# A routed feed-forward kernel on one core: three of batch 5's row scatters issued ahead of a weight split instead of behind it, in GpSimd's queue

## The reference

```python
x = x + attention(layernorm(x))       # one causal head, Wq, Wk, Wv (256 x 256), softmax(scores / 16)
x = x + ffn(layernorm(x))

def ffn(x):
    shared = down(silu(gate(x)) * up(x))                 # inner width 512
    probs = sigmoid(x @ router_w.T + routing_bias)       # 8 experts
    scores, indices = top_k(probs, 2); scores /= sum(scores)
    combined = sum over the 2 chosen experts of score * down_e(silu(gate_e(x)) * up_e(x))
    return shared + combined
```

## Time and profile before

| what | value |
|---|---|
| median of 3 runs | 569.48 us |
| lowest, highest | 565.53, 570.84 us |
| time of the profiled execution | 570.84 us |
| its span | 568.7 us |
| TensorE matmul busy | 519.9 us (91% of the span) |
| VectorE, ScalarE, GpSimd busy | 365.0, 301.2, 289.4 us |
| mean granted TensorE clock | 0.982 of full speed |

### The profile page before, as it was taken

One profiled execution on the slowest core, in us unless ns is written; L12 is line 12 of the kernel. 1 busy time (PEld: TensorE's weight loads), 2 busy tenths in 40 slices (PEclk: granted clock), 3 DMA queues, 4 the chain that ended last, 5 costly groups with the idle time before them and its releaser, 6 DMA issues. The chain is left out here.

```text
span 568.7 us, 14884 instructions
## 1 busy us (share of the span) xinstructions
PE 519.9 (91%) x4757; PEld 425.7 (75%) x4757; DVE 365.0 (64%) x962; ACT 301.2 (53%) x580; POOL 289.4 (51%) x241
## 2 busy tenths in 40 slices
PE   4889888999999999977899899999999999999980
PEld 4556677887878788866677688888788888888870
DVE  4788977889878788886456455445454454455540
ACT  3889787778777576733244344433433433344440
POOL 3456767677666666754123335334443525344353
PEclk9899999999999999989999999999999999999995
DMA  8789859969595937433455664664855645445533
GB/s 263 192 183 195 175 131 174 210 158 225 144 203 127 200 87 172 149 104 95 141 91 86 83 112 62 96 78 64 105 71 71 87 63 76 62 56 77 77 39 37
DMA packets 139350, 68.54 MB, mean 121 GB/s; under 512 B 114608, under 2 KB 132336, under 8 KB 139280
## 3 DMA queue, kind: packets, MB, share of 16 engines
q1 hardware_dynamic: 126128, 48.84, 41.8%
q0 software_dynamic: 13152, 18.76, 19.7%
HBM read 19.46 MB, written 23.08 MB: 75 GB/s over the span
## 5 line engine op out<-in xcount | busy, mean ns | idle before, releaser
L2169 PE MATMUL bank<-xn2t,w 128*128 128x256 f16 x1608 | 184.9, 273 | 3.9 <-DVE th L1635 2.1
L2169 PEld LDWEIGHTS bank<-xn2t,w 128*128 (+1 forms) x1608 | 155.0, 98 | 27.2 <-issue 3.9
L2193 PE MATMUL bank<-w,h 128*128 (+1 forms) x768 | 93.4, 276 | 0.6 <-DVE h L1452 0.5
L1626 DVE SCALAR_TENSOR_TENSOR th<-th,bank 128x512 f32<-128x512 f32 x83 | 56.6, 682 | 57.4 <-ACT th L971 53.0
L925 ACT ACTIVATE h<-th 128x512 f16<-128x512 f32 (+1 forms) x69 | 42.9, 622 | 83.9 <-DVE th L1635 75.7
L971 ACT ACTIVATE th<-bank 128x512 f32<-128x512 f32 x83 | 49.1, 592 | 66.5 <-PE bank L2169 43.1
L2193 PEld LDWEIGHTS bank<-w,h 128*128 128x128 f16 x768 | 74.8, 99 | 11.6 <-issue 1.3
L848 POOL DMA_INDIRECT out<-p,wm x28 | 44.9, 1605 | 70.8 <-ACT p L1305 21.6
L720 POOL TENSOR_TENSOR w<-wst,w 128x768 f16<-128x768 f32 x36 | 59.3, 1650 | 30.0 <-ACT w L925 29.5
L1452 DVE TENSOR_TENSOR h<-th,h 128x512 f16<-128x512 f32 (+1 forms) x69 | 47.1, 682 | 39.7 <-ACT h L925 35.4
L744 POOL DMA_INDIRECT rows<-xrow,sidx x56 | 56.3, 1005 | 15.5 <-issue 13.4
(11 more groups left out here) (193 smaller groups left out, 808.4 us busy)
## 6 DMA issues: line engine op xcount, KB each, us to landing
wst<-w_all SPq DMA_DIRECT2D x36, 384.0 KB
x<-x SPq DMA_DIRECT2D x8, 512.0 KB, 6.3
out<-x SPq DMA_DIRECT2D x8, 512.0 KB
rows<-xrow POOLq DMA_DIRECT2D x1, 1192.5 KB, 7.5
rows<-xrow,sidx POOLq DMA_INDIRECT x56
out<-p,wm POOLq DMA_INDIRECT x28, 4.1
xn2t<-rows SPq DMA_TRANSPOSE x26
wm<-rows SPq DMA_DIRECT2D x26, 9.0 KB
```

The source lines that it names most:

```text
L1626: d.scalar_tensor_tensor(out=tb, in0=tb, scalar=1.0, in1=G[half][:, :], op0=ALU.add, op1=ALU.mult).then_inc(f_sg, 1)
L2169: ins = mm(dst, w_ap(j, ws, m * MAT + k * I + (2 * half + i) * P, P), moving(ms * KD + k), start=(cnt == 0), stop=(cnt == 3 * KD - 1))
L2193: ins = mm(o[:, a * D:(a + 1) * D], hb[:, (hs * KI + i) * TT + a * P:(hs * KI + i) * TT + (a + 1) * P], w_ap(j, ws, 2 * MAT + i * D, D), s ...
```

## The change

It is made in GpSimd's list alone. Three scatters of batch 5 (m = 4, 5, 6) go ahead of `w_low(29)`, and the last (m = 7) stands between `w_low(29)` and `w_low(30)`; behind `w_low(30)` none is left. The number of instructions is the same.

```diff
--- before
+++ after
@@ -825,11 +825,10 @@
             scatter(5, 0, 1)
             xn2_low(6, 1)
             w_low(28)
-            scatter(5, 1, 4)
+            scatter(5, 1, 7)
             w_low(29)
-            scatter(5, 4, 5)
+            scatter(5, 7, 8)
             w_low(30)
-            scatter(5, 5, 8)
             last_identity()
             rstd2(7)
             table_iota()
```

## The result

| | before | after |
|---|---|---|
| median of 4 runs, us | 567.50 | 576.69 |
| lowest to highest, us | 564.42 to 570.84 | 572.58 to 578.10 |
| profiled execution, us | 570.84 | 575.28 |
| its span, us | 568.7 | 573.2 |
| granted clock, mean | 0.982 | 0.977 |

The ratio is 1.0157, with a 95% interval of 1.0113 to 1.0202. The forecast was 569.6 us, "no difference", with a range up to 572.5. The sign is clear; the size is less so, since it rests on four executions of each kernel.

What follows compares the result with a forecast made beforehand. TensorE was taken to bound the kernel, its list having hardly a gap. To the median of 569.48 us came 0.1 us for delayed transposes, all other terms 0: 569.6 us, no difference, range 565.5 to 572.5.

Steps and rivals of the forecast that it cites:

- GpSimd's pace: Six scatters from 212.74 us, one every 1.27 us; one held about 0.3 us, ending near 220.4, which costs nothing.
- The transposes: Batch 7's probabilities, before `pv(7)`: last transpose delayed 1.13 us, TensorE waits 0.1, bound 2.8; as slower rival 572.3 us, chance 0.12.
- GpSimd held back: Moved scatters take 1.40 us each, `w_low(29)` starts 1.0 us late and holds VectorE's cast: 570.5 us, chance 0.09.
- `rstd` freed: GpSimd's `rstd2(7)`, at 229.50 us, shortens without a scatter before it; TensorE gains 0.18 us at 231.76: 569.3 us, chance 0.09.
- `w_low(29)` bound by ScalarE at 220.50, cost 0: GpSimd's split still waits for ScalarE's high half of chunk 29 and starts at 220.58 as before, 0.4 us to spare.
- Here the change costs: Moved scatters enter full DMA engines at 216.3 to 222.0 us, moving that stretch's end by at most 1.13 us; TensorE waits 0.1.
- the room of the last transpose: Before the last 12 `pv` matmuls, near 223.4 us: the last transpose could land 1.0 us later without delaying TensorE.
- the pause at 258 to 264 us: TensorE's loss of 2.5 us beside batch 7's scatters might go if it depends on how transfers fall: 567.0 us, chance 0.10.

Runs made afterwards that it cites:

- with the waits: Changed kernel with waits for landing so that no more than three scatters run in a row in any batch: 569.46 us, ratio 0.9984.
- the burst of four: Changed kernel with four scatters instead of six ahead of `w_low(29)` and three instead of one behind it: 575.08 us in one execution.

## Why the prediction was wrong

*GpSimd's pace*: right. I allowed 0.3 us for one held scatter; none was held.

*The transposes*: not tested by the change. The `pv` block is unbroken and doesn't wait for `ptr`, but it started 6.6 us late. The last two transposes did get slower, 3.08 us for both in place of 2.59. In the run with six scatters spaced by 2.2 us, where `pv` started on time, the block took 3.38 us in place of 3.11, with a wait for `ptr` in it: a few tenths, near the 0.1 us of the forecast and far from its bound of 2.8.

*The rival "GpSimd held back"*: none of the six was held, and the cast took 0.55 us as before. Its other half, a late split that holds VectorE, came in the runs that took the pause away (2.41 us in place of 0.19 with the waits).

*`rstd` freed*: rightly given no gain. `rstd2(7)` still takes 1.41 us.

*`w_low(29)` bound by ScalarE at 220.50, cost 0*: the form held, the time did not. Its release came 5.4 us late, because ScalarE got the signal of sums that were complete near 217.6 only at 222.9, at the end of TensorE's pause. I had treated the release as fixed.

*The step that failed* is the head of the DMA paragraph, "Here the change costs", with the price taken from the DMA engines' share (12.6% of 9 us, 1.13 us) and from the room of the last transpose. The cost of three more scatters in a row wasn't their traffic: with half the rows the pause was 3.3 of 4.0 us. It was the run of six itself: 4.04 us of pause in the logits, 0.72 us in their pieces and 1.27 us at the lower clock behind them, 6.0 us where I had put 0.1. The sum let scatters reach TensorE only through `ptr`, and its bound from above (2.8 us) stood for that path alone. That the dense run sets off the pause is shown: cut in two by a wait (1.0036), or slowed to 2.2 us a scatter (one execution), the six leave the logits whole; with GpSimd kept busy without scatters they are whole too.

*The rival "the pause at 258 to 264 us"* had the right mechanism in view and the wrong sign. I asked whether that pause might go, and wrote "In reverse, no row says a new pause could not come" without a price. The trace held it: the largest pause without a releaser lies beside the longest run of scatters, and a run of only four, batch 4's, has 1.1 us of pauses behind it. A new run of six beside TensorE should have been a rival of its own, priced at batch 7's 2.5 us, at 572 us and more, with a chance well above 0.12.

Of the 9.2 us between the medians, the profiles show 6.6 at the `pv` block and 8.1 at the first routed matmul. Between these two the longer pause in batch 7 adds 1.3 us (3.75 against 2.46) and the slow group behind it 1.65; but the kernel before had a slow group of its own, 4.45 us from 251.08, which takes 2.78 in the changed kernel and gives 1.67 back. Why batch 7's pause grew with scatters that the change doesn't touch is open. So is the resource that the scatters share with TensorE and with its signals: the runs show what triggers the pause and what cures it. Every execution here was also recorded, so no run tells whether the recording has a part in the pauses.

## What to carry over

A stall that the profile puts down to "issue" in the middle of a block of matmuls had its cause on another engine here: look for what runs beside it each time, and price every edit that makes more of it. On this kernel four or more scatters in a row from GpSimd, at one every 1.27 us, can break up TensorE's blocks and make its signals late. A wait for landing inside every longer run made the kernel before 0.7 and 1.5% faster in two timings; 0.3 us of other work behind each scatter of batches 6 and 7 did 1.2%, but was too little beside batch 5, where the DMA engines are full. Such a wait isn't free either: in the changed kernel it made a split late, and that held VectorE. Idle time of an engine is no free place for DMA issues only because the engine is free.

## What the runs showed of the hardware

- Pauses of TensorE begin some 5 us behind the first scatter of a run at 1.27 us spacing when small matmuls are on (219.65 - 1.43 against 213.32: 4.9 us; 4.7 us with the burst of four), and end 1.3 to 2.2 us behind the end of the last (220.49 against 219.16; 222.79 against 220.64). Beside matmuls of 109 ns the first pause came 8.1 us into batch 7's eight in the kernel before, 6.5 us in the changed kernel, and 4.5 us into batch 4's four (187.75 against 183.23).
- During a pause matmuls come singly or in small groups, often 0.7 or 1.4 us apart, and TensorE's signal for work done before the pause isn't seen by ScalarE until its end (5.55 us). In the run cut in two, VectorE got such a signal 1.9 us late though no matmul block was broken. VectorE's small steps on the routing table, which wait for no other engine, ran on beside batch 7's pause in the changed kernel, from 265.0 to 267.3.
- 128 increments of a semaphore by TensorE delayed its first matmul by 13.8 us, 0.11 us each beyond what idle time hid.
- A pause of 3.75 or 4.0 us was followed by a granted clock of 0.50 and a group of 24 matmuls in 4.43 and 4.05 us instead of 2.78; one of 2.46 us wasn't. Behind the same wait of 2.71 us for VectorE the kernel before ran such a group in 4.45 us (granted clock 0.50 from 253 to 255) and the changed kernel in 2.78.
- Two small VectorE steps that met a GpSimd split of weights ended with it: 1.31 us instead of 0.15 (to 226.59, the split to 226.56) and 2.41 instead of 0.19 (to 228.97, the split to 228.91).
